# Gate products of the recurrence: plain float32 against rounded part and rest in three products

## The reference

```
# s: recurrence
x_conv = causal_depthwise_conv(xn, conv_w) + conv_b       # 4 taps
r_t = sigmoid(x_conv @ W_r.T + b_r)                       # the two gate products
i_t = sigmoid(x_conv @ W_i.T + b_i)
a_t = sigmoid(log_a) ** (8 * r_t)
h   = scan(a_t * h + sqrt(1 - a_t**2) * i_t * x_conv)
s   = rmsnorm(h @ W_out.T) * gamma
# g: twice
x = x + local_attention(shift(x) @ wqkv) @ wo
a, g = split(layernorm(shift(x)) @ w1 + b1)               # 2 x 341 hidden channels
x = x + (a * gelu(g)) @ w2 + b2
```

## Time and profile before

| | |
|---|---|
| device time, 3 runs | median 1300.65 us (1300.61 to 1301.16) |
| profiled execution | span 1302.3 us; no other time is given for it |
| PE busy | 1259.0 us (97%) |
| PEld busy | 1007.6 us (77%) |
| ACT busy | 1160.9 us (89%) |
| POOL busy | 1138.8 us (87%) |
| DVE busy | 1093.2 us (84%) |
| TensorE clock granted | full (9 of 9 tenths) in all 40 slices |

### The profile page before, as it was taken

The page is one execution under the profiler, slowest core; times in us unless marked ns, Lnnn a source line. Parts: engine busy times, 40 slices in busy tenths (PEclk is TensorE's granted clock), DMA queues, the critical chain, the costliest instruction groups (busy, mean ns, idle before and its releaser), DMA issues.

```text
span 1302.3 us, 38176 instructions
## 1 busy us (share of the span) xinstructions
PE 1259.0 (97%) x13795; PEld 1007.6 (77%) x13795; DVE 1093.2 (84%) x1883; ACT 1160.9 (89%) x3529; POOL 1138.8 (87%) x840
## 2 busy tenths in 40 slices
PE   7999999999999999899989999999999999999997
PEld 4778888888888887667657888888888888876776
DVE  7888888888888887689878898898888998874777
ACT  5889999999999999777778999999999999998886
POOL 5999999999999988378779999999999999994776
PEclk9999999999999999999999999999999999999999
DMA  5222222222222221010011222222222222110223
GB/s 168 54 63 63 62 62 63 62 63 65 68 66 67 55 62 47 17 54 1 1 29 39 47 46 46 46 47 46 50 48 59 47 46 46 39 38 25 72 75 97
DMA packets 59258, 70.04 MB, mean 54 GB/s; under 512 B 7232, under 2 KB 37376, under 8 KB 59072
## 3 DMA queue, kind: packets, MB, share of 16 engines
q1 hardware_dynamic: 59072, 67.61, 20.8%
HBM read 13.33 MB, written 4.19 MB: 13 GB/s over the span
## 4 chain that ended last, share of the span: by engine, by line
PE 71%; POOL 11%; DVE 6%; issue 6%; ACT 5%; DMA 0%; DVEq 0%; SPq 0%; ACTq 0%; POOLq 0%
PE ps L209 57%; PE ps L272 7%; POOL t L1293 5%; PE ps L285 3%; PE ps L282 3%; ACT P L674 2%; POOL P L1293 2%; POOL hxr L1293 2%; DVE t L1003 2%; POOL side L1323 1%; DVE t L1014 1%; DVE nm L1033 1%; DVE B L1074 1%; DMA norm<-X 0%; ACT sqk L648 0%
## 5 line engine op out<-in xcount | busy, mean ns | idle before, releaser
L674 ACT ACTIVATE P<-ps,nm 128x128 f32<-128x128 f32 x1024 | 363.4, 383 | 0.4
L209 PE MATMUL ps<-wqkv,hT 128*128 128x512 f32 x1152 | 330.1, 427 | 15.7 <-DVE t L1003 12.9
L1293 POOL TENSOR_TENSOR t<-t 128x1024 f32<-128x1024 f32 x128 | 307.0, 2398 | 26.1 <-DVE t L1003 24.3
L1293 POOL TENSOR_TENSOR P<-P,rden 128x512 f32<-128x512 f32 x256 | 289.9, 1143 | 19.3 <-DVE rden L1040 18.1
L209 PEld LDWEIGHTS ps<-wqkv,hT 128*128 128x128 f32 x1152 | 214.5, 188 | 95.8 <-issue 28.0
L1293 POOL TENSOR_TENSOR t<-t,rr 128x1024 f32<-128x1024 f32 x128 | 244.0, 1907 | 19.3 <-ACT rr L657 19.1
L674 ACT ACTIVATION_READ_ACCUMULATOR P<-ps,nm 128x1 f32 x1024 | 229.8, 224 | 0.0
L1014 DVE TENSOR_TENSOR t<-ps,tabl 128x512 f32<-128x512 f32 x256 | 164.1, 683 | 41.8 <-ACT sqk L648 40.6
L1293 POOL TENSOR_TENSOR hxr<-hxf,hxr 128x512 fp32r<-128x512 f32 (+1 forms) x93 | 129.0, 1413 | 71.6 <-ACT hxr L732 71.6
L664 ACT ACTIVATE PT<-ps 128x1024 f32<-128x1024 f32 x128 | 130.4, 1019 | 52.8 <-PE ps L272 51.7
L1033 DVE TENSOR_REDUCE nm<-ps 128x4 f32<-128x512 f32 x256 | 173.8, 681 | 3.9 <-PE ps L209 3.8
(11 more groups left out here) (142 smaller groups left out, 2545.3 us busy)
## 6 DMA issues: line engine op xcount, KB each, us to landing
Vs<-Vn SPq DMA_DIRECT2D x224, 128.0 KB, 2.4
side<-in_x SPq DMA_DIRECT2D x17, 256.0 KB, 3.0
A<-X SPq DMA_DIRECT2D x16, 256.0 KB, 2.5
norm<-X SPq DMA_DIRECT2D x32, 128.0 KB, 2.2
norm<-X SPq DMA_DIRECT2D x32, 127.8 KB, 2.4
hsh<-X SPq DMA_DIRECT2D x31, 128.0 KB, 2.3
hsh<-X SPq DMA_DIRECT2D x31, 127.8 KB, 2.4
oT<-in_x SPq DMA_DIRECT2D x15, 256.0 KB, 3.0
```

The source lines that it names most:

```text
L209: return e.matmul(o, lhsT, rhs, start=start, stop=stop, skip_group_check=True)
L674: k = act(P[:, g, :], ps[:, 3 + s, (g % 4) * 128:(g % 4 + 1) * 128], ACT.Exp, bias=nm[:, g:g + 1], accum_out=den[:, g:g + 1])
L1293: return e.tensor_tensor(o, a, b_, op)
```

## The change

Weights W_r and W_i are split once into a rounded part and a rest (wrr); each of the first fifteen convolved sequences is split likewise (cvr, one buffer for rounded part and rest, in the room where the attention's t1 and t2 lay). ACT makes the rounded parts, `round_wr` once and `round_cv(b)` for each sequence; DVE makes the rest of the weights once (`rest_wr`), POOL the rest of each sequence (`rest_cv(b)`). Each gate product of these fifteen sequences becomes three float32r matmuls; sequence 15 keeps the plain ones. `gates(b)` on PE now waits for POOL's rest (s_cvlo) instead of DVE's last tap (s_cv). `round_cv(b+1)` stands on ACT right behind `gates2(b)`, and waits for DVE's last tap of sequence b+1 and for `gates2(b)` of PE. `rest_cv(b)` stands at the head of POOL's turn b. DVE's first write to t2 in layer 1 waits for the last product that reads cvr.

```diff
@@ -85,7 +85,8 @@
         with ExitStack() as phase:
             room = sp_("room", [128, L])
-            sp_("kept", [128, 2048 - L])
+            wrr = sp_("wrr", [128, 2, 2, 128], F32R)
+            cvr = sp_("cvr", [128, 2, L], F32R)
             hnr = sp_("hnr", [128, 2, 2, L], F32R)
             hxf = sp_("hxf", [128, 3, L])
             hxr = sp_("hxr", [128, 2, 2, 3, L], F32R)
...
@@ -422,9 +423,20 @@
                     k = mm(ps[:, bank, :], w2r[0:n, 0, j, :], hxr[0:n, b % 2, 1, j, :], False, j == 2)
                 k.then_inc(s_y, 1)
+            def gate_product(b, g):
+                if b == NB - 1:
+                    return mm(ps[:, 7, :], wr[:, g, :], cv[b % 2])
+                for j, (p, q) in enumerate(THREE):
+                    k = mm(ps[:, 7, :], wrr[:, q, g, :], cvr[:, p, :], j == 0, j == 2)
+                return k
+
             def gates(b):
-                e.wait_ge(s_cv, 3 * (b + 1))
+                if b == NB - 1:
+                    e.wait_ge(s_cv, 3 * (b + 1))
+                else:
+                    e.wait_ge(s_cvlo, b + 1)
                 if b == 0:
+                    e.wait_ge(s_wrlo, 1)
                     e.wait_ge(s_o, NT)
                 elif b == 1:
                     e.wait_ge(s_hc, NB)
@@ -432,11 +444,11 @@
                     e.wait_ge(s_rv, NB)
                 else:
                     e.wait_ge(s_ti, b)
-                mm(ps[:, 7, :], wr[:, 0, :], cv[b % 2]).then_inc(s_gr, 1)
+                gate_product(b, 0).then_inc(s_gr, 1)
             def gates2(b):
                 e.wait_ge(s_r, b + 1)
-                mm(ps[:, 7, :], wr[:, 1, :], cv[b % 2]).then_inc(s_gi, 1)
+                gate_product(b, 1).then_inc(s_gi, 1)
             def end_turn(b):
                 e.wait_ge(s_xf, NB + b + 1)
@@ -738,6 +750,18 @@
                 elif b:
                     e.wait_ge(s_xi, b - 1)
                 act(cv[b % 2], seq(A, b), ACT.Identity, scale=cw[3], bias=CB).then_inc(s_cv0, 1)
+
+            def round_wr():
+                e.wait_ge(s_tpk, NT)
+                act(wrr[:, 0, :, :], wr[:, 0:2, :], ACT.Copy).then_inc(s_wrhi, 1)
+
+            def round_cv(b):
+                if b == 0:
+                    e.wait_ge(s_add, NT)
+                else:
+                    e.wait_ge(s_gi, b)
+                e.wait_ge(s_cv, 3 * (b + 1))
+                act(cvr[:, 0, :], cv[b % 2], ACT.Copy).then_inc(s_cvhi, 1)
             def gates(b):
                 e.wait_ge(s_gr, b + 1)
@@ -862,11 +886,14 @@
                         e.wait_ge(s_dcy, 1)
                         act(ez, ax, ACT.Exp, scale=-1.0).then_inc(s_ez, 1)
                     if l == 0 and i == NT + 2:
+                        round_wr()
                         e.wait_ge(s_dcy, 2)
                         act(lnu, u, ACT.Ln).then_inc(s_lnu, 1)
                 if l:
                     root_var(l, NB - 2)
                     rec_rms()
+                else:
+                    round_cv(0)
                 for b in range(NB + 3):
                     if 0 < b < NB:
@@ -902,6 +929,8 @@
                             e.wait_ge(s_ua, 3 * NB)
                             square(1, 0)
                         gates2(b)
+                        if b + 1 < NB - 1:
+                            round_cv(b + 1)
                     if l and b < NB - 1:
                         rec_scale(b)
                     if b == 1:
@@ -1007,6 +1036,8 @@
                     e.wait_ge(s_sq, n + 1)
                     if n:
                         e.wait_ge(s_add, n)
+                    if n == NT:
+                        e.wait_ge(s_gi, NB - 1)
                     if l and i == 0:
                         e.wait_ge(s_tabm1, 1)
                     elif l == 0 and i < TPB:
@@ -1133,6 +1164,10 @@
                     else:
                         e.wait_ge(s_cv0, b + 1)
                     e.scalar_tensor_tensor(y[:, 3 - j:], x[:, :L - 3 + j], cw[j], y[:, 3 - j:], ALU.mult, ALU.add).then_inc(s_cv, 1)
+
+            def rest_wr():
+                e.wait_ge(s_wrhi, 1)
+                e.tensor_tensor(wrr[:, 1, :, :], wr[:, 0:2, :], wrr[:, 0, :, :].bitcast(F32), ALU.subtract).then_inc(s_wrlo, 1)
             def gates2(b):
                 e.wait_ge(s_ti, b + 1)
@@ -1252,6 +1287,7 @@
                     if l and i == NT + 3:
                         rec_sum(NB - 1)
                 if l == 0:
+                    rest_wr()
                     e.wait_ge(s_gam, 16)
                     ts1(gam[:], gam[:], 0.5, ALU.mult).then_inc(s_gh, 1)
                 proj_add(l, NB - 1, 1, 2)
@@ -1354,6 +1390,10 @@
                 m = l * NB + b
                 e.wait_ge(s_hnhi, m + 1)
                 tt(hnr[:, b % 2, 1, :], seq(B, b), hnr[:, b % 2, 0, :].bitcast(F32), ALU.subtract).then_inc(s_hnlo, 1)
+
+            def rest_cv(b):
+                e.wait_ge(s_cvhi, b + 1)
+                tt(cvr[:, 1, :], cv[b % 2], cvr[:, 0, :].bitcast(F32), ALU.subtract).then_inc(s_cvlo, 1)
             def split_hx(l, b, j):
                 m, n = l * NB + b, CH[j][1]
@@ -1440,6 +1480,8 @@
                     if i == NT + 1:
                         split_hn(l, 0)
                 for b in range(NB + 3):
+                    if l == 0 and b < NB - 1:
+                        rest_cv(b)
                     if 0 <= b - 1 < (NB - 1 if l else NB):
                         for j in range(3):
                             split_hx(l, b - 1, j)
```

More of the change, by code:

```diff
@@ L192, in program @@
                                "s_hnhi", "s_gl", "s_r", "s_ti", "s_w2hi", "s_hxhi", "s_cv0", "s_h0hi"))
-        s_dec, s_rt0, s_rt, s_osq, s_rms0, s_rms, s_s, s_th = (
-            sem(n_) for n_ in ("s_dec", "s_rt0", "s_rt", "s_osq", "s_rms0", "s_rms", "s_s", "s_th"))
+        s_dec, s_rt0, s_rt, s_osq, s_rms0, s_rms, s_s, s_th, s_wrhi, s_cvhi = (
+            sem(n_) for n_ in ("s_dec", "s_rt0", "s_rt", "s_osq", "s_rms0", "s_rms", "s_s", "s_th", "s_wrhi", "s_cvhi"))
         s_cst, s_tabm, s_t2, s_ss0, s_ss, s_nm, s_rd, s_kt, s_wlo, s_w2lo, s_h0, s_hxlo1 = (
@@ L199, in program @@
             sem(n_) for n_ in ("s_bn", "s_st", "s_dcy", "s_dk", "s_xadd", "s_hc", "s_hn", "s_b1g", "s_gh", "s_oa"))
-        s_hxf, s_xf, s_cv, s_xi, s_a2n, s_hs, s_osum, s_eg, s_em, s_eo = (
-            sem(n_) for n_ in ("s_hxf", "s_xf", "s_cv", "s_xi", "s_a2n", "s_hs", "s_osum", "s_eg", "s_em", "s_eo"))
-        s_zero, s_nmr, s_nrm, s_add, s_tn, s_pn, s_hi, s_h, s_hnlo, s_a2, s_in, s_hxlo, s_wlo1, s_tabm1, s_pm, s_po = (
-            sem(n_) for n_ in ("s_zero", "s_nmr", "s_nrm", "s_add", "s_tn", "s_pn", "s_hi", "s_h", "s_hnlo", "s_a2", "s_in", "s_hxlo", "s_wlo1", "s_tabm1", "s_pm", "s_po"))
+        s_hxf, s_xf, s_cv, s_xi, s_a2n, s_hs, s_osum, s_eg, s_em, s_eo, s_wrlo = (
+            sem(n_) for n_ in ("s_hxf", "s_xf", "s_cv", "s_xi", "s_a2n", "s_hs", "s_osum", "s_eg", "s_em", "s_eo", "s_wrlo"))
+        s_zero, s_nmr, s_nrm, s_add, s_tn, s_pn, s_hi, s_h, s_hnlo, s_a2, s_in, s_hxlo, s_wlo1, s_tabm1, s_pm, s_po, s_cvlo = (
+            sem(n_) for n_ in ("s_zero", "s_nmr", "s_nrm", "s_add", "s_tn", "s_pn", "s_hi", "s_h", "s_hnlo", "s_a2", "s_in", "s_hxlo", "s_wlo1", "s_tabm1", "s_pm", "s_po", "s_cvlo"))
         def tensor(e):
```

## The result

The changed kernel takes 1331.81 us (median of 4 runs, 1329.63 to 1333.69), the kernel before 1300.63 us beside it (1300.49 to 1301.16). The ratio is 1.0227, 95% interval 1.0212 to 1.0242: slower, 31.2 us. The forecast was 1326.5, with 1316 to 1336 as its range.

What follows compares the result with a forecast made beforehand. PE was taken to bound the kernel, but the copy's wait would close a longer loop, 9.64 us against 7.95 a turn. Added to 1302.3, 25.9 us gave 1328.2 profiled, 1326.5 for the median, range 1316 to 1336.

Steps and rivals of the forecast that it cites:

- The loop: Layer 0 feed-forward: ACT's copy, POOL's rest and chunks, DVE's hidden instruction and taps, back to ACT: 9.64 us a lap.
- The rule on the port: POOL beside DVE: the later of two instructions sharing the ports is fully blocked; rest and chunks 5.7 us, not 5.52.
- The sum by the page: POOL's rest and three hidden chunks by the skill's exclusive-lock rule: 5.7 us instead of 5.52.
- ACT's wait: ACT's copy waits on DVE's taps about 1.7 us a turn, 15 to 20 us in all.
- busy share in the stage: PE in layer 0's feed-forward stage: busy share falls from all of it to about 80%.
- The rival of 1295.9: Feed-forward stage: PE stays the bound and the change gains 4.8 us, giving 1295.9; chance 0.05.
- Turns with more on POOL: Turns 3, 7, 8 and 9: 1.25 us extra for turn 9, 1.0 for each of the others.
- The second rival: Feed-forward stage: DVE's taps keep up, only first turns cost 2 to 5 us, about 1304; chance 0.05.
- The loop through PE alone: Copy, POOL's rest and chunks, PE's products, second tanh: 7.84 us, priced as today's turn.
- The sum: Whole feed-forward stage: first turns, 11 laps of 106.0 us and 4.75 for extras put turn 14's second tanh 25.9 later.

Runs made afterwards that it cites:

- e1_plain: Changed kernel with split and all waits kept, but every gate product is the plain float32 one: 1327.17 us, ratio 1.0203.
- e2_stale: Changed kernel with only sequence 0 split; copies and rests of sequences 1 to 14 left out, three products kept: 1307.74 us, ratio 1.0048.
- e9_dve: Changed kernel with the rest of cv on DVE, second tanh in PSUM, copy behind hidden chunks 0 and 1: 1317.80 us, ratio 1.0130.
- e3_nowait: Changed kernel with copy and rest reading constant columns of wo, so the copy doesn't wait for DVE's taps: 1322.85 us, ratio 1.0158.
- e4_reorder: Changed kernel with hidden chunks 0 and 1 rounded ahead of the second tanh, POOL's rest before its third chunk: 1324.62 us, ratio 1.0186.
- e5_reorder_plain: Kernel before with hidden chunks 0 and 1 rounded ahead of the second tanh; no split of cv, plain products: 1320.14 us, ratio 1.0148.
- e6_half: Changed kernel with the copy behind rounding of hidden chunks 0 and 1, POOL's rest between its chunks 0 and 1: 1328.66 us, ratio 1.0212.
- e10_gap: e2_stale's kernel with POOL's additional work in turns 3, 7, 8 and 9 held until DVE's taps are done: 1307.51 us, ratio 1.0051.
- e12_nowait_gap: e3_nowait's kernel with POOL's additional work in turns 3, 7, 8 and 9 held until DVE's taps are done: 1320.81 us, ratio 1.0147.

## Why the prediction was right, and where its sizes were off

- **The loop.** Forecast 9.64 a lap, 9.53 in the chain. Copy to POOL 0.71 (0.70 forecast), rest and chunks 5.36 (5.52), DVE's hidden instruction and gaps as forecast, taps 2.50 in the chain (2.47). The chunks run without a slow one, since DVE now waits while they run; the rest is the slow one, 1.61 beside DVE's product.
- **The rule on the port.** The rest takes 1.61 where POOL's like took 1.29 alone: 0.32 more. It starts 0.23 behind DVE's product (661.73 to 662.42), which has 0.46 left. The Trainium skill (SBUF — State Buffer, section "SBUF: two separate sides") has the second of two such instructions fully blocked while the first holds the ports, which would be all of the 0.46; the row agrees in direction and shows less, and the measured 0.32 decides. The sum by the page (5.7) was further from 5.36 than my own.
- **ACT's wait.** The second tanh starts 7.33 to 7.36 behind the copy (7.25), and ACT waits 1.48 to 1.51 for the tap (1.7). From turn 3 to 14 these waits come to 21.9 us and in the whole stage to 24.4 (15 to 20), since in the four turns with more on POOL they are 2.4 to 2.6.
- **PE.** Its busy share in the stage is 88%, and the forecast had about 80%: that was 33 matmuls by the distance between ends, 7.6 us a turn, while the view counts 8.65 of a plain turn's 9.50 as busy. Three products 0.70 from end to end (0.69); e1_plain shows that it has room, e2_stale and e9_dve that 0.3 a turn is there for a kernel whose turn PE sets. The rival of 1295.9 fell because it wasn't such a kernel any more.
- **Turns with more on POOL.** 10.45 + 10.52 + 10.56 + 10.62 less 4 x 9.51 is 4.1 us, forecast 4.25 for these four. The copy of turn 3 starts at 561.56 (564.15 forecast); 2.5 of that is an earlier start of the whole stage, in code that is unchanged.
- **The second rival's size.** The loop through PE alone was priced at 7.84, "today's turn". e3_nowait has 8.52: the term that failed is rest and chunks at 5.52, which are 5.95 there, since without the wait DVE's taps fall beside POOL; 0.2 of the difference stays unexplained. The same coupling made e4_reorder, e5_reorder_plain and e6_half miss. It was in the earlier trace rows (a product of 1.60) and in the earlier trace rows (taps of 4.63), and I had used it as a small addition only.
- **The sum.** The stage got 25.3 longer, forecast 25.9; in that, turn 15 took 10.85 instead of 9.88, +1.0, which I had as before, and the turns ahead of it 1.5 less than I had. That 25.3 is so near to 25.9 is in part luck: the two errors go against each other. Outside the stage I had put nothing: the changed profile has 2.5 less ahead of it and 4.9 more behind it. Of the latter 1.7 is one transfer, norm<-X, that took 4.08 us from issue to landing at 1212.5 instead of 2.34 before; 1.5 is a stretch of PE at its lower clock, at 1231.9 (last section); the other 1.7 is small slips. 25.3 - 2.5 + 4.9 = 27.7, the difference of the spans (1330.0 and 1302.3).
- **The median.** The medians differ by 31.2, so 3.5 more than the spans. The changed kernel's profiled execution had 2.2 us around its span and stood 0.4 above its median. If the kernel before has the same 2.2, its profiled execution took 1304.5, 3.9 above its median: an estimate, and 3.9 - 0.4 = 3.5. Its trace fits with that: its first second tanh comes at 538.99, the second latest of the fourteen profiles (533.46 to 539.66). The 5.3 us by which 1326.5 was too low are these 3.5, the 2.4 outside the stage, and -0.6 in it.

What stays open: why unchanged stretches move by some microseconds. The attention of layer 0 ended 2.2 to 2.5 us earlier in the changed kernel's profile. But e2_stale and e10_gap have the same instructions up to the first second tanh, and it comes at 539.66 in the one and at 533.46 in the other, so 2.5 us need not be an effect of the change. Turn 1 takes 10.5 to 11.7 us in the five profiles in which PE kept its clock, and 12.4 to 14.4 in the nine in which it fell; why it falls in one kernel and not in another wasn't tested.

## What to carry to other kernels

Before work is moved off the busiest engine, follow the loop that the new wait closes: the new instruction in an engine's queue, what stands behind it there, who waits for that, and whether it comes back; where the lap is longer than the busiest engine's turn, it is the turn, whatever the busy shares say. The engine that makes the new operand matters (here 0.68 on DVE against 1.29 to 1.61 on POOL): e9_dve, with the rest on DVE and the copy behind what others wait for, was the one version with the whole split that had plain turns as short as PE allows. Even so it stayed 1.3% over the kernel before, by its first turns and those with more on POOL; so work out these turns too, and not only the plain one. When POOL's and DVE's two-input instructions are put side by side, price them together: what leaves the lap on the one comes back as a longer instruction on the other.

## What the runs showed of the hardware

- A DVE instruction with two SBUF inputs can be held up for much longer than one POOL instruction: 6.06 us in e2_stale, 6.64 and 7.29 in e3_nowait, 4.27 in e9_dve, while POOL ran several two-input instructions without a gap. In e2_stale and e9_dve it ended 0.56 and 0.55 behind the last of these. With a gap on POOL (e10_gap, e12_nowait_gap) no tap was over 1.85. What the ports do inside wasn't measured.
- TensorE's granted clock was at its lower level (1.2 GHz) for stretches of 3.4 us in the changed kernel, at 569.7, 702.8 and 1231.9, and nowhere in the profile of before until its very end. The first cost nothing that the stage shows, as PE had room there. Behind the second the distance to the profile of before is no longer than ahead of it. The third cost 1.5 us: PE had waited 0.73 for POOL's chunk and 0.30 for hnr, and then took 5.95 us for eighteen matmuls that took 4.42 in the profile of before:

```profile
1231.98 5.95 PE L210 MATMUL ps<-hnr,w1r 128*128 128x512 f32 x18 [0.30 <-POOL hnr L1329]
```

- The same is the price of a slow turn 1. e3_nowait and e12_nowait_gap have the same instructions up to the end of that turn, and PE waits 2.89 us for a piece of the layer norm on DVE in both. Then its clock stays at the upper level in the one and falls in the other. PE's timelines of the nine matmuls behind that wait, and the windows view of turn 1 (columns as in the earlier trace rows; the third figure from the end is the mean granted clock), first e3_nowait's, then e12_nowait_gap's:

```profile
542.84 2.26 PE L210 MATMUL ps<-hxr,w2r 128*128 128x512 f32 x9
```

```profile
534.18:545.85 11.67, 8.74 (x35) 5.93 (x33) 10.42 (x11) 6.92 (x12) 7.57 (x5) 1.00 0.12 31
```

```profile
544.69 3.43 PE L210 MATMUL ps<-hxr,w2r 128*128 128x512 f32 x9
```

```profile
535.64:548.83 13.19, 10.26 (x35) 7.05 (x33) 11.49 (x13) 7.03 (x12) 7.57 (x5) 0.87 0.09 27
```

That is 1.5 us, and between the changed kernel and e1_plain it is 1.6 (11.53 and 13.15), in which some 0.3 can be the plain products. Every turn of over 12 us, in all fourteen profiles, has such a stretch in it, and in each of those shown here PE had been waiting ahead of it.

- Over the changed kernel's four runs the mean granted clock is 0.992 in the slowest (1333.69), 0.995 and 0.994 in the next two, and 0.997 in the fastest (1329.63).
